# K, Q and V projections replaced by two quadratic forms and a Gram matrix over the tokens

## The reference, cut to what matters

```python
h = (x - mean(x)) / sqrt(var(x) + 1e-5)                # [4096, 1024] of one batch element
q, k, v = split(h @ Wqkv + bqkv, 3)
q = q / norm(q);  k = k / norm(k)                      # per token, over 1024 columns
kv = sum over tokens of (k * v)                        # [1, 1024]
x2 = x + (q * kv) @ Wout + bout
z = layer_norm(layer_norm(x2)) * g1 + beta1
f = gelu(z @ ternary(w1).T + b1)                       # hidden width 4096
out = x2 + (layer_norm(f) * g2 + beta2) @ ternary(w2).T + b2
```

## Time and profile before

| what | value |
|---|---|
| median of 3 runs | 1505.38 us (1503.05 to 1506.87) |
| the profiled execution | 1503.7 us |
| its span on the slowest core | 1502.2 us (cores 1494.4 to 1502.2) |
| TensorE matmul busy | 1429.4 us, 95% |
| VectorE, ScalarE, GpSimd busy | 964.5, 735.9, 752.7 us |
| granted TensorE clock | 0.985 to 0.987 of full speed |
| HBM read, written | 135.37 MB, 33.55 MB |

### The profile page before, as it was taken

How to read it: one execution, slowest core, us unless ns; L and a number is a source line. 1 busy time by engine, 2 the same in 40 slices (tenths; PEclk the granted TensorE clock), 3 DMA queues, 4 the chain that set the end, 5 groups by cost and what they waited for, 6 DMA issues and landing times.

```text
span 1502.2 us, 22587 instructions; the slowest of 8 cores (1494.4 to 1502.2 us)
## 1 busy us (share of the span) xinstructions
PE 1429.4 (95%) x6848; PEld 659.8 (44%) x6948; DVE 964.5 (64%) x1536; ACT 735.9 (49%) x1142; POOL 752.7 (50%) x453
## 2 busy tenths in 40 slices
PE   5899799989999898999999999999999999999998
PEld 2444344434444443444444444444444444444443
DVE  3677669838989886842942942952952952962961
ACT  2376668668777764621721731731731730730730
POOL 2234233356565553751961960960960970970870
PEclk9999899999999999999999999999999999999999
DMA  9599999547687752002002002002002002002001
GB/s 189 143 260 274 271 275 291 194 130 247 203 242 222 219 196 99 1 29 84 1 29 85 1 29 84 1 30 84 1 26 87 1 17 88 10 15 86 13 14 44
DMA packets 53121, 162.01 MB, mean 108 GB/s; under 512 B 6149, under 2 KB 6153, under 8 KB 53001
## 3 DMA queue, kind: packets, MB, share of 16 engines
q10 hardware_dynamic: 29810, 84.53, 18.6%
q1 hardware_dynamic: 18584, 67.65, 13.2%
q0 software_dynamic: 4608, 8.39, 3.6%
HBM read 135.37 MB, written 33.55 MB: 112 GB/s over the span
## 4 chain that ended last, share of the span: by engine, by line
PE 76%; DMA 10%; DVE 5%; DVEq 3%; issue 3%; ACT 2%; POOL 1%; ACTq 1%; POOLq 0%; SPq 0%
PE y1p L791 30%; PE y2p L807 29%; DMA wst<-w1t 6%; PE kvps L650 5%; PE patt L750 4%; PE q0ps L695 2%; PE q1ps L695 2%; DMA wkv<-wqkv 2%; DVE z1T L976 1%; DMA wst<-w2t 1%; DVEq L992 1%; DVEq L855 1%; DVE xr L988 1%; DMA xr<-x 1%; DVE stA L854 1%
## 5 line engine op out<-in xcount | busy, mean ns | idle before, releaser
L791 PE MATMUL y1p<-z1T,w1q 128*128 128x512 bf16 x2001 | 454.0, 381 | 9.0 <-ACT h4r L607 5.2
L417 POOL TENSOR_TENSOR accq<-accq,sqb 128x512 f32<-128x512 f32 x248 | 423.0, 1706 | 51.1 <-ACT sqb L595 18.1
L807 PE MATMUL y2p<-w2q,h4T 128*128 128x512 fp8e4 x2048 | 444.6, 379 | 0.0
L607 ACT ACTIVATE h4r<-y1p,cols_sb,mc 128x512 bf16<-128x512 f32 x256 | 197.0, 770 | 331.1 <-PE y1p L791 323.2
L1029 DVE TENSOR_SCALAR h4T<-h4r,cols_sb 128x512 bf16<-128x512 bf16 x256 | 297.8, 1163 | 51.2 <-ACT h4r L607 50.7
L791 PEld LDWEIGHTS y1p<-z1T,w1q 128*128 128x128 fp8e4 x2048 | 195.0, 98 | 267.8 <-issue 49.8
L807 PEld LDWEIGHTS y2p<-w2q,h4T 128*128 128x128 bf16 x2048 | 200.5, 98 | 239.7
L650 PE MATMUL kvps<-wkv,z1T 128*128 128x512 bf16 x999 | 231.1, 387 | 1.3 <-issue 0.2
L595 ACT ACTIVATE sqb<-h4r 128x512 f32<-128x512 bf16 x256 | 160.3, 626 | 89.1 <-POOL accq L417 88.7
L1049 DVE SCALAR_TENSOR_TENSOR x2r<-y2p,sB,x2r 128x1024 f32<-128x1024 f32 x32 | 41.1, 1284 | 233.9 <-PE y2p L807 233.3
L414 POOL COPY accq<-sqb 128x512 f32<-128x512 f32 x8 | 7.0, 877 | 347.6 <-ACT sqb L595 347.6
(11 more groups left out here) (102 smaller groups left out, 1138.6 us busy)
## 6 DMA issues: line engine op xcount, KB each, us to landing
xr<-x SPq DMA_DIRECT2D x64, 512.0 KB, 5.7
wst<-w1t ACTq DMA_DIRECT2D x52, 512.0 KB, 7.1
wst<-w2t ACTq DMA_DIRECT2D x32, 512.0 KB, 6.2
x2scr<-xr ACTq DMA_DIRECT2D x32, 512.0 KB, 4.0
wst<-w2t ACTq DMA_DIRECT2D x64, 256.0 KB, 4.2
x2r<-x2scr SPq DMA_DIRECT2D x32, 512.0 KB, 3.3
out<-x2r SPq DMA_DIRECT2D x32, 512.0 KB, 2.6
wst<-w1t ACTq DMA_DIRECT2D x24, 256.0 KB, 4.7
```

The lines of the kernel that those rows point to most:

```text
L417: aqd.inc(gp.tensor_tensor(out=a, in0=a, in1=b, op=ALU.add))
L607: gld.inc(sc.activation(out=h4r[:, (m % 4) * 512:(m % 4 + 1) * 512], in_=y1p[m % 2][:, :], func=AF.Gelu, scale=mc[:, 0:1], bias=cols[:, C_ ...
L791: mm = te.matmul(out=y1p[m % 2][:, :], lhsT=w1q[:, c * H + m * 128:c * H + (m + 1) * 128], rhs=z1T[:, c * T + g * 512:c * T + (g + 1) * 51 ...
L807: mm = te.matmul(out=y2p[t % 2][:, hh * 512:(hh + 1) * 512], lhsT=h4T[:, m * 512 + i * 128:m * 512 + (i + 1) * 128], rhs=w2q[:, m * D + hh ...
```

## The change

It uses algebra. With M = Wk Wk', |k|^2 = h M h'; likewise for q. With G the sum over tokens of h' h / |k|, kv is the diagonal of Wk' G Wv. And (q * kv) Wout = h (Wq diag(kv) Wout). The biases are folded in: each normalised token gets a constant 0.0625 added, and each weight row (transposed weights are now the input) gets a constant that makes the product come out as with the bias.

- **New start.** 16 chunks of Wk' and Wq' (512 KB, f32) come through the weight ring on ScalarE's queue; VectorE sums each chunk's rows (`row_sum`), ScalarE writes it as bf16 with a per-row constant (`consume`). TensorE forms the upper triangles of both M in four `sweep`s over PSUM, and ScalarE and VectorE copy them into `U` between sweeps, off-diagonal blocks doubled.
- **Token loop.** For each tile `norm_mm` makes h U for k and for q (12 pieces, 4608 columns each); VectorE multiplies by h and sums (`k_norm`, `q_norm`, now scalar_tensor_tensor from PSUM with a sum output). ScalarE takes the roots (the fourth root for k), VectorE the reciprocals, GpSimd scales h by 1/sqrt(|k|) in place. In three of every four steps from step 4 on, `gram` makes four of the 12 pieces of the triangle of G for the group of four tiles before, and VectorE adds each into `gacc` (`gram_add`). ScalarE, not VectorE, now copies the transposes (`evac_t`). Eight Wv' chunks are transposed on the way. 77 chunks pass here instead of 84.
- **Between.** The last Gram group, its transposes (`g_transposes`), G Wv and its row-wise product with Wk' (128 matmuls, kv comes as a sum output), scaling of `wout` rows by kv, then 128 matmuls for Wq diag(kv) Wout (`wp`), beside which 16 chunks are rounded.
- **Attention loop.** Only `attn` on `z1T` with `wp`; no Q, no squares. 43 whole chunks are rounded in tiles 0 to 28. `z_evac` alternates: even tiles VectorE, odd tiles ScalarE, two tiles late, with two PSUM buffers. Column sums are spread over the tiles.
- w1 is handed over so that each chunk is one contiguous block.

The diff, cut to its core:

```diff
-    wseq = [("m1", i) for i in range(32)] + [("m2", i) for i in range(18)]
...
+    of_start = [("wk", i) for i in range(8)] + [("wq", i) for i in range(8)]
+    rest = iter([("m1", i) for i in range(32)] + [("m2", i) for i in range(32)]
+                + [("q", i) for i in range(64)])
+    n_tok = 8 + 64 + NQ1
+    of_step = []
+    for j in range(NT):
+        n = n_tok * (j + 1) // NT - n_tok * j // NT
+        part = [("wv", j - 6)] if 6 <= j < 14 else []
+        of_step.append(part + [next(rest) for _ in range(n - len(part))])
+    of_wp = [[next(rest) for _ in range(2)] for d in range(8)]
+    n_att = 64 - NQ1 - 16
+    of_att = [[next(rest) for _ in range(n_att * (t + 1) // 29 - n_att * t // 29)] if t < 29 else []
+              for t in range(NT)]
...
+    pieces = ([(c, lo, hi) for c in range(4) for lo, hi in ((128 * c, 512), (512, 1024))]
+              + [(c, 128 * c, 1024) for c in range(4, 8)])
...
         @block.gpsimd
+            for j in range(NT):
+                gp.wait_ge(krd.h, j + 1)
+                gp.wait_ge(nqd.h, j + 1)
+                gp.wait_ge(tpd.h, j + 1)
+                hsc.inc(gp.tensor_scalar(out=hslot(j), in0=hslot(j), ...))
+            gp.wait_ge(gfl.h, NP * NG)
+            for e in range(8):
+                wol[e].inc(gp.dma_start(out=wout[:, e * D:(e + 1) * D], ...))
...
         @block.scalar
             for j in range(NT):
                 mine = of_step[j]
+                if j + 2 < NT:
+                    ln_std(j + 2, 1.0, eps1)
+                consume(mine[0])
+                k_root(j)
+                if j + 1 < NT:
+                    evac_t(j + 1)
+                consume(mine[1])
+                q_root(j)
+                if mine[0][0] == "wv":
+                    evac_v(mine[0][1])
+                for w in mine[2:]:
+                    consume(w)
+                if j + 2 < NT:
+                    h_norm(j + 2)
...
+            for t in range(NT):
+                for w in of_att[t][:1]:
+                    consume(w)
+                if t >= 2 and t % 2 == 1:
+                    z_evac_a(t - 2)
+                ln_std(NT + t, 1.0 + EPS, cst[:, 1:2])
                 x2s[t % 4].inc(sc.dma_start(out=rows(x2_d, t), in_=xslot(NT + t)), 16)
+                for w in of_att[t][1:]:
+                    consume(w)
+                z1_norm(t)
...
         @block.tensor
+            sweep(0)
+            transposes(0)
+            for s in range(1, 4):
+                sweep(s)
             for j in range(NT):
+                te.wait_ge(hev.h, j + 1)
+                te.wait_ge(nkd.h, j) if j >= 1 else None
+                nkm.inc(norm_mm(j, nk, 0))
+                if j + 1 < NT:
+                    transposes(j + 1)
+                te.wait_ge(nqd.h, j) if j >= 1 else None
+                nqm.inc(norm_mm(j, nq, 4608))
...
+                if j >= 4 and j % 4 < 3:
+                    for p in range(4 * (j % 4), 4 * (j % 4) + 4):
+                        gram(j // 4 - 1, p)
...
+            for t in range(NT):
+                attn(t)
+                for w in of_att[t - 1] if t >= 1 else []:
+                    if w[1] >= 32:
+                        column_sums(w[1] - 32)
                 if t >= 2:
+                    z_transposes(t - 2)
...
         @block.vector
             for j in range(NT):
+                k_norm(j)
+                for kind, ch in of_step[j - 1] if j >= 1 else []:
+                    if kind == "q":
+                        clip(ch)
+                if j + 2 < NT:
+                    rstd(j + 2, SHIFT)
+                q_norm(j)
+                k_recip(j)
+                if j >= 4 and j % 4 < 3:
+                    for p in range(4 * (j % 4), 4 * (j % 4) + 4):
+                        gram_add(j // 4 - 1, p)
...
+                q_recip(j)
                 if j + 3 < NT:
+                    stats_x(j + 3)
+                if j + 1 < NT and of_step[j + 1][0][0] == "wv":
+                    row_sum(of_step[j + 1][0])
...
+            for t in range(NT):
...
+                for w in of_att[t][:1]:
+                    clip(w[1])
                 dv.drain()
                 stats(NT + t)
+                if t >= 2 and t % 2 == 0:
+                    z_evac(t - 2)
+                for w in of_att[t][1:]:
+                    clip(w[1])
+                rstd(NT + t, 0.0)
```

More of the change, by code:

```diff
@@ L478, in _ @@
[L478 to L487 removed]
+                if n >= 8:
+                    sc.wait_ge(gpm.h, NP * ((n - 8) // 4 + 1))
@@ L585, in _, with z_evac_a @@
-            ln_std(2 * NT - 1, 1.0 + EPS, cst[:, 1:2])
-            store_x2(NT - 1)
-            z1_norm(NT - 1)
+            def z_evac_a(t):
+                sc.wait_ge(zpm.h, t + 1)
+                for c in range(8):
+                    last = sc.activation(
+                        out=z1T[:, c * T + t * 128:c * T + (t + 1) * 128],
+                        in_=zps[1][:, c * 128:(c + 1) * 128], func=AF.Identity,
+                        scale=cols[:, C_G1 + c:C_G1 + c + 1],
+                        bias=cols[:, C_B1L + c:C_B1L + c + 1])
+                zva.inc(last)
@@ new lines, in gram @@
+            def gram(g, p):
+                k = NP * g + p
+                c, lo, hi = pieces[p]
+                if p == 0:
+                    te.wait_ge(hsc.h, 4 * g + 4)
+                if k >= 2:
+                    te.wait_ge(gfl.h, k - 1)
+                for i in range(4):
+                    h = hslot(4 * g + i)
+                    mm = te.matmul(out=gps[k % 2][:, 0:hi - lo],
+                                   lhsT=h[:, c * 128:(c + 1) * 128], rhs=h[:, lo:hi],
+                                   start=(i == 0), stop=(i == 3))
+                gpm.inc(mm)
@@ new lines, in _ @@
+            for d in range(8):
+                if 1 <= d <= 2:
+                    te.wait_ge(kvd.h, 6 + d)
+                if d >= 3:
+                    te.wait_ge((wpa if (d - 3) % 2 == 0 else wpv).h, (d - 3) // 2 + 1)
+                for e in range(8):
+                    if d == 0:
+                        te.wait_ge(wsd.h, e + 1)
+                    for hh in range(2):
+                        mm = te.matmul(out=wp_half(d, hh),
+                                       lhsT=wqT[:, e * D + d * 128:e * D + (d + 1) * 128],
+                                       rhs=wout[:, e * D + hh * 512:e * D + (hh + 1) * 512],
+                                       start=(e == 0), stop=(e == 7))
+                wpm.inc(mm)
@@ L713, in column_sums @@
+            def column_sums(r):
+                te.wait_ge(qd.h, 32 + r + 1)
+                if r == 0:
+                    te.wait_ge(gbd.h, 1)
+                for hh in range(2):
+                    mm = te.matmul(out=qps[hh][0:4, :],
+                                   lhsT=gb4[:, r * 4:(r + 1) * 4],
+                                   rhs=w2q[:, r * D + hh * 512:r * D + (hh + 1) * 512],
+                                   start=(r == 0), stop=(r == 31))
+                if r == 31:
                     csm.inc(mm)
@@ L780, in y1_mm @@
+            for t in range(NT - 2, NT):
+                z_transposes(t)
             def y1_mm(g, m):
@@ new lines, in _ @@
+            stats_x(0)
+            for c in range(1, 3):
+                row_sum(wx[c])
+            rstd(0, SHIFT)
+            for c in range(3, 7):
+                row_sum(wx[c])
+            stats_x(1)
+            row_sum(wx[7])
+            row_sum(wx[8])
+            row_sum(wx[9])
+            rstd(1, SHIFT)
+            sweep_evac(0)
+            for c in range(10, 14):
+                row_sum(wx[c])
+            sweep_evac(1)
+            for c in range(14, 16):
+                row_sum(wx[c])
```

1039 lines of the change are left out of this document (459 added, 580 removed).

## The result

The changed kernel takes 1593.26 us (median of 4 runs, 1586.59 to 1605.07) where the kernel before takes 1504.59 (1503.05 to 1506.87): a ratio of 1.060, with an interval of 1.053 to 1.066. Slower was right. The size was not: 1525 had been said with a range to 1552, so 68 us are to be explained. They took 21 us longer over the feed-forward part, which makes that execution 12 us longer than the median.

A forecast was written before the change was run, and what follows sets the result against it. TensorE was taken to lead, the other engines one step behind. The stages put the third feed-forward chunk at 603.4 us instead of 583.0; +20.4 on 1503.7 gives 1524, stated as 1525, range 1490 to 1552.

The forecast's parts named there:

- Feed-forward stays: From the third feed-forward matmul chunk to the end: 919 us that the change doesn't touch.
- TensorE alone gains 53 us: TensorE's own work: 331 us of matmuls removed, 273 us and 5 us of transposes added; other engines decide the gain.
- Start 62 us: From the kernel's start to the first norm product: 62 us, range 54 to 70.
- with wq6 and wq7 consumed, the last part of sweep 2 is at 49: In the start: sweep 2 ends at 49 us, once the last two wq chunks are scaled.
- Token loop 245 us: Token loop: 8.2, 7.9 and 7.4 us per Gram step, row sums of Wv' and clips added, 245 us.
- Between, 68: From the token loop to the first attention matmul: last Gram group, G Wv, row products and `wp`, 68 us.
- Attention loop 226: From the first attention matmul to the third feed-forward chunk: 226 us, where the kernel before took 270.
- The handshake: Attention loop: VectorE's first clip waits for ScalarE's z1_norm and rounding; even tiles 8.0 us, odd tiles 6.0.
- the lock: VectorE and GpSimd share a port pair, held exclusively for a whole instruction; priced at 0.2 us per attention tile.
- that addition stays at one per tile, so 0.2 more per tile: Attention loop: GpSimd's 2.5 us addition, once per tile, delays VectorE's clips by 0.2 us per tile.
- Slower still: Rival, chance 0.16: sum output or PSUM write costs extra and chunk waits add, 1553 us, if `k_norm` exceeds 1.5 us.
- The loop runs free: Rival, chance 0.1: the attention loop runs at VectorE's busy 6.1 us per tile, 22 us less, 1503 us.

The follow-up runs named there:

- the first repeat: The changed kernel run again unaltered as a yardstick, beside the kernel before: 1590.79 us, ratio 1.058.
- the small addition: The kernel before, with GpSimd adding the output bias in one column of 1024 only: 1491.7 to 1496.1 us, ratio 0.988.
- two edits: The changed kernel with the next tile's first rounding ahead of the norm and the output bias added on TensorE: 1525.09 us, 1.008 of before.
- four edits: The changed kernel with sweep copies first, V's transposes last, rounding ahead of the norm, output bias on TensorE: 1504.30 and 1505.83 us.

## Why the prediction was wrong

- *Feed-forward stays.* Right: 915 us in the repeated traces, 919 before.
- *TensorE alone gains 53 us and the others don't let it have them.* Right, and strongly: eight more matmuls per tile cost 2 us.
- *Start 62 us.* 72.0 to 76.6. The step that failed is "with wq6 and wq7 consumed, the last part of sweep 2 is at 49". It took sweep 2 as limited by its input, and left out that ScalarE's list puts the copy of sweep 1 behind the scaling of four chunks. I had followed the same list for sweep 0 (4.5 us) and stopped there. Putting the copies first gave 5 to 6 of the 10 us.
- *Token loop 245 us.* The steps were right where nothing else came in. In the first repeat the k norm products start at

```profile
272.03 2.11 PE L621 MATMUL nk<-umat,z1T 128*128 128x512 bf16 x12 [0.83 <-ACT z1T L432]
...
280.55 2.11 PE L621 MATMUL nk<-umat,z1T 128*128 128x512 bf16 x12
...
288.40 2.11 PE L621 MATMUL nk<-umat,z1T 128*128 128x512 bf16 x12
```

  and then at 295.85 and 301.19, or 8.5, 7.9, 7.4 and 5.3 us for the predicted 8.2, 7.9, 7.4 and 5.8: 29.2 against 29.4. The next four take 30.1, with 9.5 for the first. Sum output and PSUM write are in the product's 1.22 us, with the nearest row at 1.23. The step that failed is the V chunks, priced at VectorE's row sums alone; the eight steps took 80.1 us for 69.9, TensorE's wait for ScalarE behind the shared transposes buffer was 15.7 us, and moving it gave 11.
- *Between, 68.* 8 over in the trace. The sum left out its own 3.5 us of idling, which was 5.7 in the trace. The last Gram group took 15.8 us where 11.3 had been counted, at a granted clock of 0.82, and G Wv 30.6 for 27.6, at 0.90; `wp` took 27.7 for 30. No experiment took this stage apart.
- *Attention loop 226.* The handshake was there, released as said. Undisturbed it takes 7.94 and 6.00 us where 7.8 and 5.8 had been counted; that the sums 8.0 and 6.0 came out to 0.06 us is luck, as their 0.2 for the lock made up for it. One term inside was short: ScalarE's eight small copies,

```profile
437.22 2.89 ACT L538 ACTIVATE z1T<-zps,cols_sb 128x128 bf16<-128x128 bf16 x8
```

  are busy 2.9 us and 2.7 to the next start (439.89), where the rows gave 2.5. The 2.0 that followed from the Trainium skill (VectorE: DVE Perf Modes, "The TRN2 errata") is too low. The step that failed is "that addition stays at one per tile, so 0.2 more per tile". It is 6.4 us for the loop; 32 to 34 were measured, and this is the largest part of the miss. Two errors lie in it. I took the lock from the clip's own row, where the one-column products beside it held as much. And I read its price under TensorE's bound: of the 30 us that the lock held VectorE before, the small addition took away 22, and the end saw at most 18. Now the loop has 29 to 35 us of it, and the end saw 34 when they went. That VectorE and ScalarE release one another by turns, so that a delay is paid in full, fits their waits above; it is argued from them.
- *Rivals.* "Slower still" had the nearer number, 1553, by a mechanism that isn't there: `k_norm` stayed at 1.22 us, under its 1.5. "The loop runs free" needed two edits and then gave 191.
- In the token and attention loops DMA was not the bound, as said (at the start VectorE did wait for chunks, 5.0 us for one of them): landing medians fell from 7.1 to

```profile
wst<-w1c ACTq DMA_DIRECT2D x64, 512.0 KB, 4.8
```

## What to carry to other kernels

When the leading engine is taken away, every wait that it hid gets its full price: reprice all delays of the engines behind it, not only their busy times. A lock is to be summed over every line of the engine it stops, the one-column ones too, as mean less median times count. And where two engines release each other by turns, follow both lists through one whole period before any figure of busy time is believed; here one moved addition and three swaps of order were worth 85 us, where the change had lost 79 on the same chip. And a stage is read on all cores: the slowest one alone gave 196.7 for a loop that took 191.

## What was not expected of the hardware

- An instruction on 128x1 operands, 0.16 us on VectorE, is held for up to 2.07 us (2.27 in a repeat) while GpSimd adds 1024 columns; with GpSimd's operand cut to one column the maximum is 0.161.
- GpSimd's scaling of 128x1024 bf16 in place takes 2.84 us, more than its f32 addition (2.35), above the upper end that I had set for it; it hid as expected but for the last one, for which TensorE waited 5.7 us.
- Two edits that cut waits in one ring gained 32 and 29 us of the loop alone and 66 together, by the medians of the cores (34 and 25 of the kernel's time alone, 66 together).
- In the attention loop the granted clock was 0.83 when TensorE was busy 111 of 160 us, 0.90 at 131, and 0.99 in the kernel with four edits (123 of 140).
